# Windowed attention, one core: each block of v spread once in rows of four heads by 32 keys, and the scores' maxima ahead of the sum of the older weights

## The chip, the core and the metric

The kernel runs on one core of one Trainium2 chip. A core has TensorE (matrix products; its weight loads are listed apart as PEld), VectorE (DVE), ScalarE (ACT), GpSimd (POOL) and SyncE (SP, which here only issues DMAs), each with its own instruction list in order. They are held together by semaphores. The metric is the device time of one execution in microseconds. The time before is 4051.28 us, the median of three runs (4048.12 to 4060.52).

## The reference

The input is x of 8 batch elements, 512 tokens, 128 dimensions, with a vector that modulates it. First comes one causal attention layer with 16 heads of 8 dimensions. Then follow six layers, each with a windowed attention and a gated feed-forward part; nearly all of the time, and the whole change but one line, is in the windowed attention:

```
q, k, v = split(x @ Wqkv)           # 16 heads of 64
q, k = rotary(l2norm(q)), rotary(l2norm(k))
# windows of 32 queries; each sees the 32 keys before it and its own 32
sim  = q_w @ [k_(w-1), k_w].T * 8, masked: i < j, i > j + 32, or before the start
out  = softmax(sim) @ [v_(w-1), v_w]          # per head
x   += out @ Wo                     # heads side by side
```

All arithmetic is float32.

## The kernel before

**Units, tiles and steps.** `local_stack` works through 48 units (6 layers by 8 batch elements). A unit has four tiles of 128 tokens (4 windows of 32). One pass of the loop body has four steps, t = 0 to 3, and each step takes a different stage of several tiles: the projections of tile n (`q`, `k`, `v0`, `v1`), the transposes and scores of tile n-1 (`tq`, `tk`, `sim`), the exponential and the normalisation of tile n-2 (`ex`), and the transpose of the weights and the product with v of tile n-3 (`pt`, `z`, `zt`). The feed-forward part of an older unit is spread over the steps: `m1` (means) in step 3, `m2` (variances) in step 0, `h` (three hidden products) in step 1, `y` in step 2. The list `jobs_of` gives TensorE's order in a step: q, tq, k, (ex), tk, v0, pt, sim, v1, z, then m1, m2, h or y, then zt. Each job names the PSUM banks it writes (`q`, `v1`, `pt` in 0 and 1, `v0` in 2 and 3, `z` in 2), and `slot_free` waits until the earlier user of these banks has been taken out.

**Where the work lies.** V is projected with Wo already folded in, so v has 128 columns for each of 16 heads. `v0` and `v1` are two halves of 8 heads, which ScalarE copies to `v_tok` (two buffers, L598, function `copy_v`). TensorE takes rows of 128 in its product with v, and a row is one head and one key. Before, `v_win` (two buffers, `par`) holds for each window 2 heads by 64 keys (the 32 keys before and its own 32) in the 128 partitions, and 8 column blocks; `z` is 8 products per window, one for each pair of heads, 32 per tile.

**SyncE.** `spread_v(u, t)` copies `v_tok` into `v_win` by DMA. Before, each block of 32 keys is written twice, as own keys and as keys before. It waits for both halves of v (`taken`), puts the last 32 keys by in `v_held` (L382, in steps 0 to 2, two issues), waits for `ready["z"]` up to tile n, takes over the older 32 keys from `v_held` (L389, two issues), and issues two times three copies of 64 partitions (L394) and one of 32 (L396). `ready["z"]` starts at 2, so this waits for z of tile n-2. `copy_v` of tile n waits in its turn until the spread of tile n-2 has landed (`win_in`) and, with three tiles of four, until `held_in`. In the last unit of a layer SyncE also loads the next layer's weights in 1 MB pieces: q's and k's ahead of the spread of step 2, v's two ahead of the spread of step 3, each when the last tile has used the old ones (L349), and behind each spread a rotary table (L367).

**VectorE's order in a step.** For q and then k: the sum of squares (L719), the product with the cosines (L723), a clamp (L730, once), two products with the sines (L737, two halves). Then the mask is added to the scores of tile n-1 (L761), then the sum of the weights of tile n-2 (L768), its reciprocal (L770) and the product (L772). In step 1 the gates of the feed-forward part (L749), which wait for ScalarE's gelu; in step 3 the subtraction of the mean (L783), for which ScalarE's square L659 waits. Then the maxima of tile n-1 (L788), the remainder of the next input (L695, steps 0 and 2), the update of x (L799), in step 2 y's (L808).

**ScalarE's order in a step.** Squares of q (L569, L571), the copy of tq, squares of k (L573), k into `k_bd` (L618), the transposed weights (L625), `copy_v(0)`, the logarithm of the norms (L580), the exponential of the scores (L633), the exponential of the norms (L586), in step 1 L640, `copy_v(1)`, the copy of z (L651), then the feed-forward part's pieces: L659 in step 3, three on m2 in step 0, a table load, three gelus and a table load in step 1.

**GpSimd.** It adds the two rotary halves of q and k (L835), refines and applies the norms (L855), and subtracts the maxima from the scores (L883) for the next step's exponential.

**The attention part in front** (`modulated_attention`) also folds Wo into v's weights, one 64-row product per head (`fold`, four groups of four heads; `vt` are the transposed weights, made in steps 2 and 3 of 16, `fold` in steps 7, 7, 11 and 14).

## Time and profile before

| | |
|---|---|
| median of three runs | 4051.28 us |
| the profiled execution, whole | 4061.07 us |
| its span (first to last instruction) | 4059.3 us |
| TensorE busy | 3598.6 us, 89% |
| VectorE busy | 3208.4 us, 79% |
| GpSimd busy | 2756.6 us, 68% |
| ScalarE busy | 2604.8 us, 64% |
| DMA | 512.39 MB, mean 126 GB/s |
| mean granted TensorE clock | 0.974 |

The attention part takes the first 750 us or so, the 48 units the rest, save some 75 us of filling, draining and the last residual. "Busy" is the time in which an engine has an instruction in it; one share over the whole span hides that each step of a unit has its own limit, so the tables below are read by step. Times in a timeline count from the start of the span. In brackets stands how long the engine had been idle before an instruction and what ended that.

### The profile page before, as it was taken

What the parts mean: (1) busy time and instruction counts of PE and PEld (TensorE: products, weight loads), DVE (VectorE), ACT (ScalarE), POOL (GpSimd) and SP (SyncE); (2) the same over time, 40 slices, a digit from 0 to 9 for tenths busy, and PEclk for the clock granted to TensorE, in tenths of its full rate; (3) what the DMA queues carried; (4) which work ended last, traced back from release to release, by engine and by line L of the source; (5) the groups of instructions that cost most, each with busy time, mean ns of one, the idle gap of its engine ahead of it and who ended that gap; (6) DMA issues with size and microseconds to landing.
All of it is one profiled execution on the core that took longest, in us unless ns stands there. A gap on an engine that the chain in (4) does not pass through costs nothing. (4 is left out here: it accounts for less than half of the span.)

```text
span 4059.3 us, 104487 instructions
## 1 busy us (share of the span) xinstructions
PE 3598.6 (89%) x39260; PEld 2658.4 (65%) x39260; DVE 3208.4 (79%) x4352; ACT 2604.8 (64%) x3817; POOL 2756.6 (68%) x2238
## 2 busy tenths in 40 slices
PE   6988888689998999989999989999899998999995
PEld 4666666467666667666766666667576666666663
DVE  5556556588897889887888888888798887888883
ACT  3555555467766676766776767677567676767763
POOL 2344343477777787777777777777677777777772
PEclk9999999799999999999999999999899999999997
DMA  1222220366666666676666676666766667666663
GB/s 47 73 75 90 72 99 16 102 146 133 139 132 164 133 148 134 133 170 133 138 137 132 133 175 139 132 132 142 166 134 137 132 134 174 133 139 134 143 136 88
DMA packets 172730, 512.39 MB, mean 126 GB/s; under 512 B 36862, under 2 KB 56444, under 8 KB 166396
## 3 DMA queue, kind: packets, MB, share of 16 engines
q1 hardware_dynamic: 172668, 511.58, 55.4%
q8 instruction: 37, 0.61, 0.1%
q14 instruction: 25, 0.20, 0.0%
HBM read 51.11 MB, written 32.51 MB: 21 GB/s over the span
## 5 line engine op out<-in xcount | busy, mean ns | idle before, releaser
L460 PE MATMUL st_ps<-st_wqkv,st_xs 128*128 128x512 f32 x4608 | 1273.3, 412 | 99.7 <-DMA st_wqkv<-wqkv_parts 56.3
L835 POOL TENSOR_TENSOR st_qk_rot<-st_qk_rot,st_qk_sq 128x1024 f32<-128x1024 f32 x384 | 912.4, 2381 | 568.4 <-DVE st_qk_sq L737 568.4
L460 PEld LDWEIGHTS st_ps<-st_wqkv,st_xs 128*128 128x128 f32 x4608 | 815.7, 190 | 336.9 <-issue 194.0
L855 POOL TENSOR_TENSOR st_qk_rot<-st_qk_rot,st_rn 128x1024 f32<-128x1024 f32 x384 | 731.2, 1925 | 15.0
L598 ACT ACTIVATE st_v_tok<-st_ps 128x1024 f32<-128x1024 f32 x384 | 389.9, 1015 | 248.5 <-DMA st_v_win<-st_v_tok 244.2
L719 DVE TENSOR_REDUCE st_nt<-st_qk_sq 128x16 f32<-128x1024 f32 x384 | 465.6, 1212 | 78.1 <-ACT st_qk_sq L571 58.1
L737 DVE TENSOR_TENSOR st_qk_sq<-st_ps,st_rot 128x512 f32<-128x512 f32 x768 | 490.0, 678 | 0.0
L723 DVE TENSOR_TENSOR st_qk_rot<-st_ps,st_rot 128x1024 f32<-128x1024 f32 x384 | 467.9, 1219 | 7.5 <-PE st_ps L475 1.6
L500 PE MATMUL st_ps<-st_v_win,st_probT 128*32 128x128 f32 x12288 | 376.1, 274 | 90.1 <-ACT st_v_tok L598 86.7
L1531 DVE TENSOR_REDUCE at_nmx<-at_s 128x1 f32<-128x512 f32 (+3 forms) x512 | 236.7, 485 | 255.1 <-PE at_s L1144 253.8
L500 PEld LDWEIGHTS st_ps<-st_v_win,st_probT 128*32 128x32 f32 x12288 | 325.1, 110 | 165.0 <-issue 155.9
L475 PE MATMUL st_ps<-consts_sb,st_qk_rot 128*128 128x128 f32 x3072 | 402.6, 274 | 11.7 <-POOL st_qk_rot L855 8.2
L475 PEld LDWEIGHTS st_ps<-consts_sb,st_qk_rot 128*128 128x128 f32 x3072 | 353.1, 141 | 87.4 <-issue 47.1
L883 POOL TENSOR_TENSOR st_s<-st_s,st_mx 128x1024 f32<-128x1024 f32 x192 | 374.3, 1949 | 48.7 <-DVE st_mx L788 48.7
L618 ACT ACTIVATE st_k_bd<-st_ps 64x1024 f32<-64x1024 f32 x384 | 389.2, 1013 | 5.1 <-PE st_ps L475 2.9
L1347 ACT ACTIVATE at_probT<-at_t 128x512 f32<-128x512 f32 (+1 forms) x384 | 201.2, 526 | 288.4 <-PE at_t L1163 282.9
L488 PE MATMUL st_ps<-st_k_bd,st_qT 128*32 128x128 f32 x12288 | 377.0, 275 | 2.5 <-ACT st_k_bd L618 2.5
L768 DVE TENSOR_REDUCE st_den<-st_ps 128x16 f32<-128x1024 f32 x192 | 235.0, 1224 | 162.6 <-ACT st_ps L633 160.5
L488 PEld LDWEIGHTS st_ps<-st_k_bd,st_qT 128*32 128x32 f32 x12288 | 325.3, 110 | 36.1 <-issue 31.8
L625 ACT ACTIVATE st_probT<-st_ps 128x1024 f32<-128x1024 f32 x192 | 196.9, 1025 | 231.2 <-PE st_ps L480 231.2
L1614 POOL TENSOR_TENSOR at_qs<-at_q,consts_sb 128x512 fp32r<-128x512 f32 x128 | 131.0, 1041 | 268.6 <-DVE at_q L1477 202.0
L480 PE MATMUL st_ps<-consts_sb,st_s 128*128 128x128 f32 x1536 | 208.9, 280 | 98.9 <-issue 97.7
(149 smaller groups left out, 6154.7 us busy)
## 6 DMA issues: line engine op xcount, KB each, us to landing
st_v_win<-st_v_tok SPq DMA_DIRECT2D x1152, 256.0 KB, 4.6
st_v_win<-st_v_tok SPq DMA_DIRECT2D x384, 128.0 KB, 4.8
st_v_held<-st_v_tok SPq DMA_DIRECT2D x288, 128.0 KB, 4.1
st_v_win<-st_v_held SPq DMA_DIRECT2D x288, 128.0 KB, 2.3
st_wqkv<-wqkv_parts SPq DMA_DIRECT2D x24, 1024.0 KB, 8.5
wqkv_parts<-at_w_parts SPq DMA_DIRECT2D x12, 1024.0 KB, 4.4
wqkv_parts<-at_fold_parts SPq DMA_DIRECT2D x12, 1024.0 KB, 4.6
at_w_raw<-in_wqkv SPq DMA_DIRECT2D x18, 512.0 KB, 5.5
```

The costliest lines, as they stand in the source:

```text
L460: last = pe.matmul(out[:, c * 512:(c + 1) * 512], xs[:, x_part, t * P:(t + 1) * P], wqkv[:, PROJ.index(kind), w_part, c * 512:(c + 1) * 51 ...
L475: last = pe.transpose(out[:, c * P:(c + 1) * P], src[:, c * P:(c + 1) * P], ident)
L488: last = pe.matmul(out[g * WIN:(g + 1) * WIN, c * P:(c + 1) * P], qT[:, par, c * P + g * WIN:c * P + (g + 1) * WIN], k_bd[:, c, :, key:key ...
L500: last = pe.matmul(out[g * WIN:(g + 1) * WIN, 0:P], probT[:, c * P + g * WIN:c * P + (g + 1) * WIN], v_win[:, par, g, c * P:(c + 1) * P], ...
L598: act.activation(v_tok[:, t % 2, a, :], slot_of(f"v{a}", 0, t), ACT.Copy).then_inc(taken[f"v{a}"], 1)
L618: last = act.activation(k_bd[rows, :, a, WIN + t1 * P:WIN + (t1 + 1) * P], src[rows, :, :], ACT.Copy)
L719: dve.tensor_reduce(nt[:, 2 + par, heads], qk_sq[:, cols].rearrange("p (h d) -> p h d", d=DH), AX.X, ALU.add).then_inc(ss_sum, 1)
L723: dve.tensor_tensor(qk_rot[:, cols].rearrange("p (h d) -> p h d", d=DH), slot_of("qk"[a], 0, t).rearrange("p (h d) -> p h d", d=DH), rot[: ...
L737: last = dve.tensor_tensor(dst[:, :, g, :], src[:, :, 1 - g, :], sines.unsqueeze(1).to_broadcast([P, HEADS, DH // 2]), ALU.mult)
L835: pool.tensor_tensor(qk_rot[:, cols], qk_rot[:, cols], qk_sq[:, cols], ALU.add).then_inc(rot_done[a], 1)
L855: pool.tensor_tensor(view, view, rn[:, par, heads_of(a)].unsqueeze(2).to_broadcast([P, HEADS, DH]), ALU.mult).then_inc(normed[a], 1)
L883: pool.tensor_tensor(scores, scores, mx[:, tt % 2, :].unsqueeze(2).to_broadcast([P, HEADS, 2 * WIN]), ALU.subtract).then_inc(shifted, 1)
```

## The change

Four parts.

1. V is spread once. `v_win` has a buffer for each of the four tiles; its 128 partitions are 4 heads by 32 keys, its 4 column blocks the other factor of the 16 heads. `spread_v` issues 16 copies of 32 partitions by 2 KB (64 KB each) per tile, all on `win_in[t]`. `v_held`, its copies and their semaphores are gone. `ready["z"]` starts at 3, so the spread of tile n waits for z of tile n-3. `z` makes 4 products per window with its own keys and then 4 with the keys before, which it reads from the window before, in the same or in the previous tile's buffer; in the first window of a unit these 4 are left out.
2. The scores lie in another order: in each PSUM bank of 512 first the 8 heads' 32 older keys, then the 8 heads' 32 own ones. `sim` reads k in that order (pieces of 32) and writes two pieces of 64. The mask is added from a table of this layout, laid out once at the start. The maxima, the sums and the product are each two instructions of 512, a bank each, and so is GpSimd's subtraction; the reduces run over two dimensions.
3. VectorE takes the maxima straight after the mask add, ahead of the sum, the reciprocal and the product of tile n-2 and of what follows these.
4. Which heads are folded into which columns changes with it; every fold group waits for both halves of the transposed weights.

From top to bottom: the layout's helpers, SyncE's `spread_v`, TensorE's `sim` and `z`, ScalarE's `copy_v` (its two waits on z follow the new start value), VectorE (the start, then the step), GpSimd, and the fold of the attention part.

```diff
-        v_win = sb("v_win", [P, 2, WPT, INNER])
-        v_held = sb("v_held", [P, INNER])
+        v_win = sb("v_win", [P, TILES, WPT, INNER // 2])
+        masks = sb("masks", [P, 2, 512])
...
+    def spread_count(u, d):
+        return u * 256 + 256 * (d + 1)
+    def bank_of(tensor, b):
+        return tensor[:, b * 512:(b + 1) * 512].rearrange("p (s h k) -> p s h k", s=2, h=HEADS // 2)
+    def heads_first(tensor, b):
+        return tensor[:, b * 512:(b + 1) * 512].rearrange("p (s h k) -> p h s k", s=2, h=HEADS // 2)
+    def per_head(tensor, b):
+        half = tensor[:, b * (HEADS // 2):(b + 1) * (HEADS // 2)]
+        return half.unsqueeze(1).unsqueeze(3).to_broadcast([P, 2, HEADS // 2, WIN])
...
-                        for a in range(2):
-                            sp.dma_start(v_held[held_rows(t, a), :], v_tok[P - WIN:P, par, a, :]).then_inc(held_in[par], 16)
                     sp.wait_ge(ready["z"], tiles_done(u, 0, t))
-                        sp.wait_ge(held_in[1 - par], held_count(u, 0, t - 1))
-                        for a in range(2):
-                            sp.dma_start(v_win[a * 2 * WIN:a * 2 * WIN + WIN, par, 0, :], v_held[held_rows(t - 1, a), :])\
-                              .then_inc(carry_in[par], 16)
...
-                        for g in range(1, WPT):
-                            sp.dma_start(v_win[rows, par, g, :], v_tok[(g - 1) * WIN:(g + 1) * WIN, par, a, :])\
-                              .then_inc(win_in[par], 16)
-                        sp.dma_start(v_win[a * 2 * WIN + WIN:(a + 1) * 2 * WIN, par, 0, :], v_tok[0:WIN, par, a, :])\
-                          .then_inc(win_in[par], 16)
+                    for g in range(WPT):
+                        for h in range(4):
+                            sp.dma_start(v_win[h * WIN:(h + 1) * WIN, t, g, :],
+                                         v_tok[g * WIN:(g + 1) * WIN, par, h // 2, h % 2 * 512:h % 2 * 512 + 512])\
+                              .then_inc(win_in[t], 16)
...
-                                            out[g * WIN:(g + 1) * WIN, c * P:(c + 1) * P],
+                                            half[:, :, c % 4 * 2 * WIN:(c % 4 + 1) * 2 * WIN],
                                             qT[:, par, c * P + g * WIN:c * P + (g + 1) * WIN],
-                                            k_bd[:, c, :, key:key + 2 * WIN], start=True, stop=True)
+                                            k_bd[:, c, :, key:key + 2 * WIN].rearrange("p a (s k) -> p s a k", s=2),
...
-                                pe.wait_ge(win_in[par], spread_count(u, d, index))
-                                if index:
-                                    pe.wait_ge(carry_in[par], carry_count(u, d, index))
+                                pe.wait_ge(win_in[index], spread_count(u, d))
+                                for s_part in (1, 0):
+                                    for c in range(4):
+                                        chunk = c // 2 * 4 + s_part * 2 + c % 2
+                                        for g in range(WPT):
+                                            t_win, g_win = divmod(index * WPT + g - 1 + s_part, WPT)
+                                            if t_win < 0:
+                                                continue
+                                            last = pe.matmul(
+                                                out[g * WIN:(g + 1) * WIN, 0:P],
+                                                probT[:, chunk * P + g * WIN:chunk * P + (g + 1) * WIN],
+                                                v_win[:, t_win, g_win, c * P:(c + 1) * P], start=(s_part == 1 and c == 0),
+                                                stop=(c == 3 and (s_part == 0 or index * WPT + g == 0)))
...
-                                act.wait_ge(win_in[t % 2], spread_count(u, d2, t2))
-                                if t2 < TILES - 1:
-                                    act.wait_ge(held_in[t2 % 2], held_count(u, d2, t2))
+                                act.wait_ge(win_in[t2], spread_count(u, d2))
...
+                for i in range(2):
+                    dve.tensor_copy(masks[:, i, :].rearrange("p (s h k) -> p s h k", s=2, h=HEADS // 2),
+                                    mask[i].rearrange("p (s k) -> p s k", s=2).unsqueeze(2).to_broadcast([P, 2, HEADS // 2, WIN]))\
+                       .then_inc(masked, 1)
...
-                                              mask[0 if t1 == 0 else 1].unsqueeze(1).to_broadcast([P, HEADS, 2 * WIN]),
+                                              masks[:, t1 > 0, :].unsqueeze(1).to_broadcast([P, 2, 512]),
                                               ALU.add).then_inc(taken["sim"], 1)
+                        if alive(u, d1):
+                            dve.wait_ge(taken["sim"], n - 1)
+                            for b in range(2):
+                                last = dve.tensor_reduce(mx[:, t1 % 2, b * 8:b * 8 + 8], heads_first(s[:, t1 % 2, :], b), AX.XY, ALU.max)
+                            last.then_inc(max_ready, 1)
                         if alive(u, d2):
                             dve.wait_ge(ready["ex"], n - 2)
-                            dve.tensor_reduce(den[:, t2 % 2, 0, :], weights, AX.X, ALU.add).then_inc(den_ready, 1)
+                            for b in range(2):
+                                last = dve.tensor_reduce(den[:, t2 % 2, 0, b * 8:b * 8 + 8], heads_first(weights, b), AX.XY, ALU.add)
...
+                            for b in range(2):
+                                last = dve.tensor_tensor(bank_of(s[:, t2 % 2, :], b), bank_of(weights, b),
+                                                         per_head(den[:, t2 % 2, 1, :], b), ALU.mult)
+                            last.then_inc(taken["ex"], 1)
...
-                        if alive(u, d1):
-                            dve.wait_ge(taken["sim"], n - 1)
-                            dve.tensor_reduce(mx[:, t1 % 2, :], scores, AX.X, ALU.max).then_inc(max_ready, 1)
...
-                for a in range(2):
-                    pool.memset(v_win[a * 2 * WIN:a * 2 * WIN + WIN, 0, 0, :], 0.0).then_inc(v_zeroed, 1)
-                pool.sem_inc(ready["z"], 2)
+                pool.sem_inc(ready["z"], 3)
...
+                            for b in range(2):
+                                scores = bank_of(s[:, tt % 2, :], b)
+                                last = pool.tensor_tensor(scores, scores, per_head(mx[:, tt % 2, :], b), ALU.subtract)
...
-                        rows, half = slice(g // 2 * DH, (g // 2 + 1) * DH), g % 2
-                        pe.wait_ge(taken["vt"], count(b, 0, 2, half))
+                        rows = slice(g % 2 * DH, (g % 2 + 1) * DH)
+                        pe.wait_ge(taken["vt"], count(b, 0, 2, 1))
...
-                            c = TILES * half + i
+                            c = 2 * i + g // 2
```

## Rows read from the trace of the kernel before

**Rows 1.** Busy time by window, one unit: window, length, then busy time and count per engine.

```profile
2014.60:2080.30 65.70, 61.10 (x730) 45.06 (x730) 57.65 (x73) 46.18 (x65) 51.53 (x41) 1.00 0.64 136
```

**Rows 2.** List of waits, whole run: who waits, for whom, us in total, times, longest.

```profile
ACT st_v_tok L598 <- DMA st_v_win<-st_v_tok: 244.2, 137, 3.4
...
DVE st_den L768 <- ACT st_ps L633: 160.5, 138, 2.9
...
ACT st_xc L659 <- DVE st_xc L783: 99.3, 48, 7.6
...
PE st_ps L500 <- ACT st_v_tok L598: 86.7, 92, 2.0
...
PE st_ps L460 <- DMA st_wqkv<-wqkv_parts: 56.3, 8, 11.1
```

**Rows 3.** Timeline, VectorE, each step's first L719: start, us, instruction, [idle before].

```profile
2010.85 1.22 DVE L719 TENSOR_REDUCE st_nt<-st_qk_sq 128x16 f32<-128x1024 f32 x1 [0.32 <-DVE xT_sb L808]
...
2025.21 1.22 DVE L719 TENSOR_REDUCE st_nt<-st_qk_sq 128x16 f32<-128x1024 f32 x1 [0.30 <-ACT st_qk_sq L571]
...
2040.85 1.21 DVE L719 TENSOR_REDUCE st_nt<-st_qk_sq 128x16 f32<-128x1024 f32 x1
...
2060.89 1.22 DVE L719 TENSOR_REDUCE st_nt<-st_qk_sq 128x16 f32<-128x1024 f32 x1 [0.66 <-ACT st_qk_sq L571]
...
2076.57 1.22 DVE L719 TENSOR_REDUCE st_nt<-st_qk_sq 128x16 f32<-128x1024 f32 x1 [0.32 <-DVE xT_sb L808]
```

**Rows 4.** Timeline of steps 0 and 1: what waits behind the spread.

```profile
2033.21 1.02 ACT L598 ACTIVATE st_v_tok<-st_ps 128x1024 f32<-128x1024 f32 x1 [2.02 <-DMA st_v_win<-st_v_tok]
...
2035.30 1.23 DVE L768 TENSOR_REDUCE st_den<-st_ps 128x16 f32<-128x1024 f32 x1 [1.59 <-ACT st_ps L633]
...
2034.47 1.95 PE L500 MATMUL st_ps<-st_v_win,st_probT 128*32 128x128 f32 x64 [0.95 <-ACT st_v_tok L598]
...
2050.08 1.95 PE L500 MATMUL st_ps<-st_v_win,st_probT 128*32 128x128 f32 x64 [0.93 <-ACT st_v_tok L598]
```

**Rows 5.** Timeline of step 2, VectorE: pair, mask add, sum, reciprocal, product.

```profile
2066.98 1.28 DVE L737 TENSOR_TENSOR st_qk_sq<-st_ps,st_rot 128x512 f32<-128x512 f32 x2
2068.18 1.21 DVE L761 TENSOR_TENSOR st_s<-st_ps,consts_sb 128x1024 f32<-128x1024 f32 x1
2069.44 1.23 DVE L768 TENSOR_REDUCE st_den<-st_ps 128x16 f32<-128x1024 f32 x1
2070.70 0.25 DVE L770 RECIPROCAL st_den<-st_den 128x16 f32<-128x16 f32 x1
2070.99 1.23 DVE L772 TENSOR_TENSOR st_s<-st_ps,st_den 128x1024 f32<-128x1024 f32 x1
```

**Rows 6.** Lines L389 and L396, SP's issues: duration in ns, least, median, most.

```profile
L389 SPq DMA_DIRECT2D st_v_win<-st_v_held x288: 507/534/601, 788.1 to 3976.7; - x144
...
L396 SPq DMA_DIRECT2D st_v_win<-st_v_tok x384: 598/1018/1997, 773.0 to 3983.4; - x192
```

**Rows 7.** Timeline of step 3: mask add, subtraction of the mean, ScalarE's square of it.

```profile
2018.13 1.21 DVE L761 TENSOR_TENSOR st_s<-st_ps,consts_sb 128x1024 f32<-128x1024 f32 x1
...
2022.60 0.68 DVE L783 TENSOR_TENSOR st_xc<-xT_sb,st_ps 128x512 f32<-128x512 f32 x1
...
2023.32 0.63 ACT L659 ACTIVATE st_xc<-st_xc 128x512 f32<-128x512 f32 x1 [1.94 <-DVE st_xc L783]
```

**Rows 8.** Timeline across a change of layer, SP and TensorE.

```profile
1257.29 1.62 PE L460 MATMUL st_ps<-st_wqkv,st_xs 128*128 128x512 f32 x6
...
1275.78 1.64 PE L460 MATMUL st_ps<-st_wqkv,st_xs 128*128 128x512 f32 x6 [1.45 <-DMA st_wqkv<-wqkv_parts]
...
1279.63 0.94 SPq L349 DMA_DIRECT2D st_wqkv<-wqkv_parts  x2
...
1289.30 2.90 PE L460 MATMUL st_ps<-st_wqkv,st_xs 128*128 128x512 f32 x6 [11.01 <-DMA st_wqkv<-wqkv_parts]
...
1300.64 1.64 PE L460 MATMUL st_ps<-st_wqkv,st_xs 128*128 128x512 f32 x6
```

More of the change, by code:

```diff
@@ L264, in local_stack @@
         wqkv_in = {k: sem(f"w{k}_in") for k in PROJ}
-        win_in = [sem("win_in0"), sem("win_in1")]
-        carry_in = [sem("carry_in0"), sem("carry_in1")]
-        held_in = [sem("held_in0"), sem("held_in1")]
-        zeroed, shift_zeroed, v_zeroed, rot_in = sem("zeroed"), sem("shift_zeroed"), sem("v_zeroed"), [sem(f"rot_in{t}") for t in range(TILES)]
+        win_in = [sem(f"win_in{t}") for t in range(TILES)]
+        masked = sem("masked")
+        zeroed, shift_zeroed, rot_in = sem("zeroed"), sem("shift_zeroed"), [sem(f"rot_in{t}") for t in range(TILES)]
         KINDS = (*PROJ, "tq", "tk", "pt", "sim", "ex", "z", "zt", "m1", "m2", "h", "y")
@@ L487, in unit @@
                                         key = index * P + g * WIN
+                                        half = out[g * WIN:(g + 1) * WIN, c // 4 * 512:c // 4 * 512 + 512].rearrange("p (s x) -> p s x", s=2)
                                         last = pe.matmul(
-                                            out[g * WIN:(g + 1) * WIN, c * P:(c + 1) * P],
+                                            half[:, :, c % 4 * 2 * WIN:(c % 4 + 1) * 2 * WIN],
                                             qT[:, par, c * P + g * WIN:c * P + (g + 1) * WIN],
-                                            k_bd[:, c, :, key:key + 2 * WIN], start=True, stop=True)
+                                            k_bd[:, c, :, key:key + 2 * WIN].rearrange("p a (s k) -> p s a k", s=2),
+                                            start=True, stop=True)
@@ L492, in unit @@
                             elif kind == "z":
                                 pe.wait_ge(taken["pt"], tiles_done(u, d, index))
-                                pe.wait_ge(win_in[par], spread_count(u, d, index))
-                                if index:
-                                    pe.wait_ge(carry_in[par], carry_count(u, d, index))
-                                for c in range(IC):
-                                    for g in range(WPT):
-                                        last = pe.matmul(
-                                            out[g * WIN:(g + 1) * WIN, 0:P],
-                                            probT[:, c * P + g * WIN:c * P + (g + 1) * WIN],
-                                            v_win[:, par, g, c * P:(c + 1) * P], start=(c == 0), stop=(c == IC - 1))
+                                pe.wait_ge(win_in[index], spread_count(u, d))
@@ L646, in unit @@
                         if alive(u, d3):
[L648 removed]
+                            act.wait_ge(ready["z"], n)
                             if not (start and n < 5):
@@ L753, in unit @@
                         d1, t1 = divmod(t - 1, TILES)
-                        scores = s[:, t1 % 2, :].rearrange("p (h k) -> p h k", h=HEADS)
                         if alive(u, d1):
@@ L760, in unit @@
                                 dve.wait_ge(ready["pt"], n - 3)
[L761 to L762 removed]
+                            dve.tensor_tensor(s[:, t1 % 2, :].rearrange("p (b x) -> p b x", b=2),
+                                              slot_of("sim", d1, t1).rearrange("p (b x) -> p b x", b=2),
+                                              masks[:, t1 > 0, :].unsqueeze(1).to_broadcast([P, 2, 512]),
                                               ALU.add).then_inc(taken["sim"], 1)
+                        if alive(u, d1):
[3 more added lines that the diff above has]
+                            last.then_inc(max_ready, 1)
                         if alive(u, d2):
                             dve.wait_ge(ready["ex"], n - 2)
[L767 to L768 removed]
+                            weights = slot_of("ex", d2, t2)
+                            for b in range(2):
+                                last = dve.tensor_reduce(den[:, t2 % 2, 0, b * 8:b * 8 + 8], heads_first(weights, b), AX.XY, ALU.add)
+                            last.then_inc(den_ready, 1)
                             dve.wait_ge(den_ready, 2 * (n - 2) - 1)
@@ L817, in _ @@
             def _(pool):
-                for a in range(2):
-                    pool.memset(v_win[a * 2 * WIN:a * 2 * WIN + WIN, 0, 0, :], 0.0).then_inc(v_zeroed, 1)
-                pool.wait_ge(v_zeroed, 2)
-                pool.sem_inc(ready["z"], 2)
+                pool.sem_inc(ready["z"], 3)
                 pool.wait_ge(small_in, 64)
```

31 lines of the change are left out of this document (3 added, 28 removed).

## The prediction

> **What bounds the kernel now.** I read the table of busy time by window first, then the list of waits, then the timeline of one unit (one of 48 passes over a layer and a batch element), engine by engine, and last the timeline across a change of layer. In one unit of 65.7 us TensorE is busy 61.1, VectorE 57.7 and ScalarE 46.2 [rows 1]. No engine is full, so the step length is set by a loop that runs through several engines, and the reader has to find the place where each step is held up.
>
> I measure a step from the start of VectorE's first reduce (L719 on q) to the same instruction of the next step: 14.36 us in step 3, 15.64 in step 0, 20.04 in step 1 and 15.68 in step 2, together 65.72 [rows 3]. The loop is this: VectorE's three instructions on q free the banks in which TensorE then puts `pt`; TensorE runs `pt`, `sim`, `v1`, `z`, the feed-forward product of that step, `zt` and the next `q`; ScalarE squares that q; VectorE reduces it. VectorE's own list is the second loop, and the longer one decides.
>
> Where the DMA stands in it: `copy_v(0)` on ScalarE waits 244.2 us over the run until the spread of tile n-2 has landed. Behind this wait queue the exponential of the scores, for which VectorE's sum then waits (160.5 us), and the release of bank 2, for which TensorE's `z` waits (86.7 us) [rows 2]. In step 0 the copy is 2.02 us late, VectorE's sum 1.59 and `z` 0.95; in step 1 `z` is 0.93 late [rows 4]. In step 2 nothing waits for the DMA, and VectorE is full: only 0.32 us of idle stands before its next L719 [rows 3]. In step 3 the copy is late, but `z` isn't.
>
> **Spreading v once, four tiles kept.** SP's condition changes from "z of tile n-2 done" to "z of tile n-3 done". z of tile n-3 runs in step n itself, so the spread starts a whole step earlier. Sixteen issues follow. The nearest row is the copy of 32 partitions from v_held, median 0.534 us per issue; the other is the last quarter of the old spread, 1.018 us, issued behind a backlog of 256 KB copies [rows 6]. I take 0.57 with the gap between two, since the new pieces (64 KB) are smaller than both and leave no backlog: 16 x 0.57 = 9.1 us per step of 14.6 us or more. Landing comes one more step ahead of the copy that waits for it. So the waits of ScalarE on this DMA go, all of them.
>
> What is late next, step by step. Step 0: `z` starts 0.95 us earlier, with it `m2`, and ScalarE's three instructions on it, its squares and L719: with some 0.08 us that TensorE's weight load waits beside it, 15.64 becomes 14.61. VectorE's own list must fit under this (below: 14.28, it does, with 0.3 us to spare). Step 1: `z` 0.93 us earlier, with it the three h products, the two table loads and gelus; with some 0.07 beside it 20.04 becomes 19.04. The maxima stood in the gap in which VectorE waits for gelu, and there is room left without them.
>
> **VectorE's order and its halved instructions.** Three 1024-wide instructions become pairs of 512. A pair with no wait between is L737, 1.28 us, against 1.21 for one 1024-wide [rows 5]: +0.07 each. L737 reads runs of 32 like the new forms, so I add nothing for the order of the elements. The maxima now stand straight behind the mask add that they depend on. A dependent pair costs 1.26 from start to start (sum, then reciprocal), the reciprocal and the product 0.29, and one without a dependence some 0.12 less than 1.26 [rows 5]. The block was mask 1.26, sum 1.26, reciprocal 0.29, product 1.14, maxima 1.13, in all 5.08 us when nothing waits; it becomes mask 1.25, maxima 1.20, sum 1.32, reciprocal 0.29, product 1.20, in all 5.26: +0.18 per tile. Bounds: 0 (a pair as dear as one), and +0.15 per pair if each half costs an unoverlapped 0.68 us; no row shows a reduce over two dimensions or with a gap, so its upper end is open and is a rival below.
> The Trainium skill ("VectorE: DVE Perf Modes", "The DRAIN you can't avoid") says that the next instruction cannot start before the pipe is empty and that the count of instructions should be kept low, which speaks against halving. The trace has the overlapped pair at +0.07 us [rows 5]; by the page it would be nearer the +0.15, and the sum some 10 us less good.
>
> Step 2 is VectorE's own: 15.68 + 0.19 = 15.87. Step 0: the mask add 7.29 after L719 [rows 3, 5], the block 5.26, and what follows it in the list (the update of x, the remainder of the next input): from the sum to the next L719 it was 2035.30 to 2040.85 without idle [rows 3, 4], 5.55, less sum, reciprocal, product and maxima (3.82), 1.73. Together 14.28.
>
> **Where the new order hurts.** In step 3 VectorE subtracts the mean (L783) for ScalarE's L659, which stands ahead of ScalarE's squares of the next q; L659 waits 99.3 us over 48 units [rows 2], 1.94 each time [rows 7]. Before, L783 stood behind the product and ahead of the maxima. Now the maxima are ahead of it: from the mask add to L783 it is 5.26 us where it was 4.47 with the 0.58 us of idle that the DMA caused (the mask add at 2018.13, L783 at 2022.60 [rows 7]). L783, L659, the squares and L719 are all 0.79 us later: 14.36 becomes 15.15. TensorE is not what ends that step, so its slack doesn't help.
>
> A unit: 15.15 + 14.61 + 19.04 + 15.87 = 64.67 against 65.72, 1.05 us less, times 48 = 50 us.
>
> **The change of layer.** At five of them TensorE waits for new weights, 56.3 us in all [rows 2], 11.3 each. SP issues v's weights only at 1279.63, because it sits in `spread_v` waiting for `z` of the current step, and then issues ten copies; TensorE starts on them at 1289.30, 9.7 us later [rows 8]. The granted clock is at its lower level (1.2 GHz) behind this wait: six products took 2.90 us against 1.64 a step on [rows 8], and by the same ratio, for part of their time, `pt` and `sim` lose another 1.3, so 2.6. Some 1.7 us of wait would be there without the weights (TensorE's `pt` waits for VectorE's L737 in any case), so a change costs 11.3 + 2.6 - 1.7 = 12.2 us. Now SP's wait is over long before. q's weights go out when q of tile 3 is done (1257.29 + 1.62 [rows 8] = 1258.9), k's 2.3 us on (1261.2), the sixteen spreads until 1270.5, the table and v's at 1271.4: 8.2 us earlier. TensorE starts on v at 1281.1; without the 1.45 us for k's weights [rows 8] and with the 1 us that `pt` waits anyway it would lose nothing until 1277.6. That leaves 3.5 us, and half of the low clock's 2.6, since the wait is a third as long: 4.8. 12.2 - 4.8 = 7.4 us, times 5 = 37. Bounds: 1 us each (issues at 1.018), 12 each.
>
> **The rest.** `sim` and `z` have the same counts, save 4 products fewer in tile 0, where TensorE waits anyway: nothing. `sim` now reads in four pieces of 32 and writes in two of 64; it already reads in two of 64 at the price of z's contiguous 128, so nothing, and up to 0.2 us per step (25 us) as a bound. GpSimd's shift in halves: like VectorE's pairs, +0.07 to 0.15 us a step; GpSimd is busy 51.5 of 65.7 us [rows 1], and its last piece of the step, the shift, is wanted only by the next step's exponential: nothing. The two mask tables cost VectorE a pair, 1.3 us, once. In the attention part the fold waits for both halves of the transposed weights, four steps after the second was made: nothing. GpSimd's two memsets went: nothing.
>
> Sum: -50 - 37 + 1 = -86 us. The profiled execution took 4061.07 us (span 4059.3), the median of the runs is 4051.28, 9.8 less: 4061 - 86 = 3975 profiled, 3965 for the median.
>
> **Rivals.**
> 1. The subtraction isn't late (VectorE catches up, or ScalarE's squares were not what ended step 3): 48 x 0.79 = 38 us more gain, 3927. For it: only one step of four. Against: L659's wait is in every unit. 0.13.
> 2. The wait on the DMA was covered: next limits stand close behind in steps 0 and 1 (GpSimd's normalising of q, the slots), the +0.79 and +0.19 eat what little goes, and only the layers' changes gain: 4051 - 37 = 4014. For it: `z` waits only in half the steps, 86.7 us in all. 0.15.
> 3. The issues keep their price of 1.018 us at the changes of layer only: 4051 - 50 - 5 = 3996. 0.07.
> 4. SP becomes the bound: at 1.018 + 0.04 us each, 64 issues take 67.7 us per unit, against the 65.72 of now: +2.0 x 48 = 96 us, 4147, slower. It decides from 0.98 us an issue. For it: the 1.018 row is a 32-partition copy too. Against: that row follows copies of 256 KB, and 0.534 is seen without these [rows 6]. 0.05.
> The Trainium skill ("DMA: Bandwidth & Descriptors", "Measured") has 64 KB transfers at 0.95 us and calls those below 64 KB dominated by descriptors; that is for another path, and would put SP just under this bound, with a time near 3996 or worse.
> 5. The new access patterns are dear: a reduce over two dimensions with a gap costs VectorE 0.6 us or more than one over 64 in a row, twice per step. +1.2 us is in full on steps 3 and 2, 0.9 on step 0, 0.6 on step 1, together 3.9 us x 48 = 187: 4152, slower. It decides from some 0.3 us per reduce. 0.08.
>
> My forecast holds 0.52. A difference counts as one from 0.3%, 12 us, on. Faster: 0.52, 0.13, 0.07 and 0.12 of rival 2 make 0.84, of which I take 0.03 off for what no row shows (the length of the loops' code, for one), 0.81; same: rival 2's other 0.03 and 0.02 of these, 0.05; slower: rivals 4 and 5 and the last 0.01, 0.14. The range of 8 in 10 reaches from rival 1 to a little past rival 2.
>
> **What would show it.** Right: no wait of L598 on a DMA; L768 without idle; `z` without a wait on ScalarE; L659's wait 2.7 us instead of 1.94, and step 3 at 15.1 while steps 0 and 1 are 1 us shorter; the SP issue near 0.55; TensorE's wait for st_wqkv some 20 us in all instead of 56. Wrong: an L768 or maxima pair above 1.4 us, `sim` above 2.1, SP's queue without gaps, or a step 3 of 14.4.

## The result and the profile after

The changed kernel takes 3945.97 us (median of four runs, 3941.92 to 3950.02) against 4051.16 for the kernel before beside it: ratio 0.9737, interval 0.9716 to 0.9757, 105 us less. The forecast was 3965. The profiled execution took 3942.58 us, 118.5 less than the 4061.07 of before.

From the page: the span, the busy times, the DMA, and the copies of v and of the weights (size of each, median us from issue to landing; before, the copies of v were 256 and 128 KB and took 4.6 and 4.8 us, the weights 8.5).

```profile
span 3940.8 us, 104815 instructions
...
PE 3568.8 (91%) x38876; PEld 2641.1 (67%) x38876; DVE 3285.9 (83%) x4930; ACT 2611.0 (66%) x3817; POOL 2784.8 (71%) x2428
...
DMA packets 181947, 285.96 MB, mean 73 GB/s; under 512 B 52222, under 2 KB 71804, under 8 KB 175612
...
st_v_win<-st_v_tok SPq DMA_DIRECT2D x3072, 64.0 KB, 2.0
st_wqkv<-wqkv_parts SPq DMA_DIRECT2D x24, 1024.0 KB, 7.0
```

The list of waits answers to [rows 2]. No wait of `copy_v` (now L584) on a DMA is in it; the sum (now L766) waits for ScalarE once; the wait of L645 (the L659 of before) has grown, as forecast.

```profile
ACT st_xc L645 <- DVE st_xc L783: 134.5, 48, 6.7
...
PE st_ps L442 <- DMA st_wqkv<-wqkv_parts: 8.2, 6, 2.3
...
DVE st_den L766 <- ACT st_ps L619: 2.7, 1, 2.7
```

One unit by window, as [rows 1], and VectorE's first reduce of each step (L719 is now L710), as [rows 3].

```profile
2003.34:2068.29 64.95, 61.00 (x723) 45.06 (x722) 59.35 (x84) 46.31 (x65) 52.15 (x46) 1.00 0.28 65
```

```profile
2003.34 1.22 DVE L710 TENSOR_REDUCE st_nt<-st_qk_sq 128x16 f32<-128x1024 f32 x1 [1.03 <-ACT st_qk_sq L559]
...
2019.03 1.22 DVE L710 TENSOR_REDUCE st_nt<-st_qk_sq 128x16 f32<-128x1024 f32 x1 [0.32 <-DVE xT_sb L804]
...
2034.18 1.22 DVE L710 TENSOR_REDUCE st_nt<-st_qk_sq 128x16 f32<-128x1024 f32 x1 [1.44 <-ACT st_qk_sq L559]
...
2049.27 1.21 DVE L710 TENSOR_REDUCE st_nt<-st_qk_sq 128x16 f32<-128x1024 f32 x1
...
2068.29 1.22 DVE L710 TENSOR_REDUCE st_nt<-st_qk_sq 128x16 f32<-128x1024 f32 x1 [1.03 <-ACT st_qk_sq L559]
```

| step | before | forecast | after |
|---|---|---|---|
| 3 | 14.36 | 15.15 | 15.15 |
| 0 | 15.64 | 14.61 | 15.09 |
| 1 | 20.04 | 19.04 | 19.02 |
| 2 | 15.68 | 15.87 | 15.69 |
| unit | 65.72 | 64.67 | 64.95 |

Here are VectorE's pairs in step 3, and ScalarE behind them: the maxima and the sum take 1.28 us a pair, with the reciprocal between sum and product, and the mean's subtraction L783 comes 5.25 us after the mask add. ScalarE waits 2.72 us for it, then squares q, and only then can L710 start.

```profile
2026.32 1.21 DVE L751 TENSOR_TENSOR st_s<-st_ps,st_masks 128x1024 f32<-128x1024 f32 x1
...
2027.57 1.28 DVE L759 TENSOR_REDUCE st_mx<-st_s 128x8 f32<-128x512 f32 x2
...
2028.76 1.28 DVE L766 TENSOR_REDUCE st_den<-st_ps 128x8 f32<-128x512 f32 x2
...
2030.07 0.25 DVE L769 RECIPROCAL st_den<-st_den 128x16 f32<-128x16 f32 x1
...
2030.36 1.29 DVE L772 TENSOR_TENSOR st_s<-st_ps,st_den 128x512 f32<-128x512 f32 x2
...
2031.57 0.68 DVE L783 TENSOR_TENSOR st_xc<-xT_sb,st_ps 128x512 f32<-128x512 f32 x1
...
2032.28 0.64 ACT L645 ACTIVATE st_xc<-st_xc 128x512 f32<-128x512 f32 x1 [2.72 <-DVE st_xc L783]
```

The change of layer, SyncE first and then TensorE (answers to [rows 8]). SyncE is no longer held by `z`; v's weights are issued at 1252.41, and TensorE's v0 starts at 1258.00 with 1.64 us of idle and at the full clock (1.63 us for its six products).

```profile
1238.66 2.59 SPq L348 DMA_DIRECT2D st_wqkv<-wqkv_parts  x2
1241.71 10.04 SPq L377 DMA_DIRECT2D st_v_win<-st_v_tok  x16
1251.79 0.58 SPq L366 DMA_DIRECT2D st_rot<-rotary_tables  x1
1252.41 0.93 SPq L348 DMA_DIRECT2D st_wqkv<-wqkv_parts  x2
```

```profile
1255.33 1.04 PE L457 MATMUL st_ps<-consts_sb,st_qk_rot 128*128 128x128 f32 x8
1258.00 1.63 PE L442 MATMUL st_ps<-st_wqkv,st_xs 128*128 128x512 f32 x6 [1.64 <-DMA st_wqkv<-wqkv_parts]
1259.47 1.04 PE L462 MATMUL st_ps<-consts_sb,st_s 128*128 128x128 f32 x8
```

**Where the time came from.** I measure from one `pt` to the `pt` four steps on. The five stretches with a change of layer fell from 394.0 us in all to 326.6: 67.4 us, which is 12.7 each beyond an ordinary unit's share. The first four stretches lost 10.2 together (3.2 of it ordinary); the late spread below gives this back, so it comes from the earlier start of the spread. The other 38 stretches lost 29.5, 0.78 each, and what follows the last of them 3.7. The attention part in front lost 7.7; two runs with the same code there (the changed kernel and the first experiment) began their first `pt` at 798.95 and 806.72, so that is no effect of the change, and it is most of why the profiled pair differs by more than the medians. The changes of layer scatter too: in two runs below that keep the old spread, the five stretches took 384.5 and 388.6 us, not 394.0. Up to 2 us of the 12.7 can be such scatter.

### The profile page after: what moved, and what is told of

Its sections match the earlier page's. It is cut to its first block and busy times, and to the rows that moved or that the text cites. A ratio compares the mean times of both kernels' runs of the same rounds, so it can differ in the third digit from the quotient of the medians.

```text
span 3940.8 us, 104815 instructions
## 1 busy us (share of the span) xinstructions
PE 3568.8 (91%) x38876; PEld 2641.1 (67%) x38876; DVE 3285.9 (83%) x4930; ACT 2611.0 (66%) x3817; POOL 2784.8 (71%) x2428
## 5 line engine op out<-in xcount | busy, mean ns | idle before, releaser
L848 POOL TENSOR_TENSOR st_qk_rot<-st_qk_rot,st_rn 128x1024 f32<-128x1024 f32 x384 | 731.9, 1927 | 15.0
L710 DVE TENSOR_REDUCE st_nt<-st_qk_sq 128x16 f32<-128x1024 f32 x384 | 466.0, 1213 | 136.4 <-ACT st_qk_sq L559 121.6
L877 POOL TENSOR_TENSOR st_s<-st_s,st_mx 128x512 f32<-128x512 f32 x384 | 404.1, 1073 | 6.0 <-DVE st_mx L759 6.0
L584 ACT ACTIVATE st_v_tok<-st_ps 128x1024 f32<-128x1024 f32 x384 | 388.0, 1010 | 3.2 <-PE st_ps L442 3.1
L462 PEld LDWEIGHTS st_ps<-consts_sb,st_s 128*128 128x128 f32 x1536 | 165.9, 141 | 204.5 <-issue 203.0
```

Source lines behind the costliest of these rows:

```text
L584: act.activation(v_tok[:, t % 2, a, :], slot_of(f"v{a}", 0, t), ACT.Copy).then_inc(taken[f"v{a}"], 1)
L710: dve.tensor_reduce(nt[:, 2 + par, heads], qk_sq[:, cols].rearrange("p (h d) -> p h d", d=DH), AX.X, ALU.add).then_inc(ss_sum, 1)
L848: pool.tensor_tensor(view, view, rn[:, par, heads_of(a)].unsqueeze(2).to_broadcast([P, HEADS, DH]), ALU.mult).then_inc(normed[a], 1)
L877: last = pool.tensor_tensor(scores, scores, per_head(mx[:, tt % 2, :], b), ALU.subtract)
```

## The experiments

Times are medians; each ratio is to the kernel before on the same chip. Unit lengths are from the profiled run of each.

**The maxima put back in the changed kernel**

```diff
 # VectorE, changed kernel
-    (mask add) (maxima) (sum, reciprocal, product) (gates) (mean's subtraction)
+    (mask add) (sum, reciprocal, product) (gates) (mean's subtraction) (maxima)
```

> The changed kernel with the maxima put back to their old place, behind the subtraction of the mean; the layout, the halves and the single spread stay. Theory A (mine): with the DMA wait gone, the exponential is ready when the mask add ends, so the sum can follow at once and the early maxima gain nothing; in step 3 they delay the subtraction for which ScalarE waits. Step 3 goes from 15.15 to 14.4 us, the others stay: 48 x 0.75 = 36 us less than 3946, so 3910. Rival B: the early maxima fill a wait of VectorE for the exponential, and without them step 0, 1 and 2 each grow by up to 1.2 us: 3946 + 48 x 1 to 3, 4000 or more. Rival C: neither matters, 3946 within 10.

Measured: 3902.96 us, ratio 0.9637 (0.9622 to 0.9653), 43 us less than the changed kernel. Step 3 is 14.01 instead of 15.15, the unit 63.78. ScalarE waits 1.58 us for the mean instead of 2.72, the same 1.14:

```profile
2014.76 1.03 ACT L619 ACTIVATE st_ps<-st_s 128x1024 f32<-128x1024 f32 x1 [0.56 <-DVE st_qk_sq L728]
...
2019.39 0.63 ACT L645 ACTIVATE st_xc<-st_xc 128x512 f32<-128x512 f32 x1 [1.58 <-DVE st_xc L777]
```

The forecast's 0.79 for this step was right against the step of before, but that step still held 0.58 us of wait for the DMA. Against the changed kernel with its old order the loss is 1.14. Over 48 units that would be 55 us, and the stretches from `pt` to `pt` do fall by 51.5; in this profiled run the attention part, whose code is the same, took 7.8 us longer, and the medians, 43 apart, hold such scatter too.

**The same reordering alone, in the kernel before**

```diff
 # VectorE, kernel before
+    maxima (dve.tensor_reduce(mx...)) ahead of the sum
-    maxima behind the mean's subtraction
```

> The kernel before with one part of the change alone: the maxima moved up, straight behind the mask add, ahead of the sum. Theory A (mine): it fills time in which VectorE waits for the exponential anyway (0.58 to 1.59 us in steps 3, 0 and 1), so these steps don't gain, since they end with ScalarE or GpSimd; in step 3 the subtraction of the mean comes 0.6 us later and the step grows by 0.6 us, in step 2 by 0.1: 48 x 0.7 = 34 us more than before, 4085. Rival B: the early maxima are a gain by themselves where the wait on the DMA is still there: 4051 - 20 or less. Rival C: the 1.14 us per unit that they cost in the changed kernel are their price here too: 4051 + 55 = 4106.

Measured: 4048.15 us, ratio 0.9988 (0.9974 to 1.0002), no change to be told; my figure, 4085, was wrong. The steps say why: 14.95, 15.0, 20.2 and 15.69 against 14.36, 15.64, 20.04 and 15.68. Step 3 loses 0.59, and step 0 gains as much. There `copy_v` still waits for the DMA and the exponential behind it is late; VectorE used to stand idle for 1.59 us before the sum [rows 4], and now the maxima fill that hole. The list of waits of this run: the copy's wait is there as before, the sum's has gone from 160.5 to 9.4, and L719 waits 173.6 us for the squares.

```profile
DVE st_nt L719 <- ACT st_qk_sq L571: 173.6, 134, 2.7
...
DVE st_den L772 <- ACT st_ps L633: 9.4, 8, 2.7
```

**The spread one step later, in the changed kernel**

```diff
-                pool.sem_inc(ready["z"], 3)
+                pool.sem_inc(ready["z"], 2)
 # and ScalarE's two waits on z one lower
```

> The changed kernel with the spread held back by one step: it waits for z of tile n-2 again instead of n-3, with the four buffers, the single spread and half the bytes kept. Theory A (mine): the gain comes from the earlier start, not from the bytes, since 16 issues of 0.63 us take as long as the old ten. The spread then lands some 12 us after z, ScalarE's copy_v(0) waits for it again some 1 to 2 us per step and the weights of v come late at a change of layer: 4030 to 4060. Rival B: half the bytes are what took the wait away, and the time stays at 3946 within 15.

Measured: 4013.47 us, ratio 0.9910 (0.9894 to 0.9926). That is 67 us more than the changed kernel, and all of it lies elsewhere than I said: an ordinary unit is 64.92 us, unchanged. The five stretches with a change of layer are 74.6 to 76.3, some 10 more each, and the first four units 14 more together. `copy_v` waits for the DMA again, but 0.21 to 0.83 us at a time instead of 1 to 2, and that is about what the exponential behind it waits for VectorE anyway (0.55 to 1.04 in the changed kernel).

```profile
ACT st_v_tok L584 <- DMA st_v_win<-st_v_tok: 102.3, 137, 3.7
...
PE st_ps L442 <- DMA st_wqkv<-wqkv_parts: 48.3, 6, 10.0
```

So with this order of VectorE the ordinary unit doesn't need the earlier start. The single spread, half the bytes in copies that land in 2.0 us instead of 4.6, brings the copy's wait from 244.2 us over the run [rows 2] down to 102.3, and what is left of it is covered. The earlier start pays at the changes of layer and at the beginning. Whether the bytes or the size of each copy count wasn't separated.

**Both of these together**

```diff
 # changed kernel with the late spread, and the maxima back behind the mean
```

> The changed kernel with the spread held back by one step (as in the second experiment, where the ordinary unit kept its 64.92 us although ScalarE's copy waited 0.6 to 0.8 us for the DMA) and the maxima in their old place (the first experiment, 63.78 us per unit). Theory A (mine): what is left of the DMA wait was covered by the slack that the early maxima made; with the maxima late the exponential is wanted earlier, and a part of the 0.6 to 0.8 us shows: a unit of 64.2 to 64.8 us, the changes of layer 10 us each: 3903 + 67 + 30 = 4000. Rival B: the late spread costs an ordinary unit nothing in either order, unit 63.8, time 3970.

Measured: 3983.2 us, ratio 0.9839 (0.9814 to 0.9863). Unit 64.17: step 3 is 14.0, but step 0 is 15.4 and not 15.07, since the sum waits for ScalarE again, 81.8 us over the run. The time lies between my figure and the rival's (4000 and 3970). In this order the earlier start is worth 0.39 us in each ordinary unit (63.78 against 64.17); the early maxima had hidden that. With the late spread the early maxima cost 30 us, with the early spread 43, and in the kernel before they cost nothing. The less VectorE waits for the exponential, the less there is for them to fill.

**v's weights behind the last spread**

```diff
-                            for kind in (("q", "k"), ("v0", "v1"))[t - (TILES - 2)]:   # ahead of spread_v(u, t)
+                            for kind in ("v0", "v1"):                                 # behind spread_v(u, TILES - 1)
```

> The changed kernel with the loads of the next layer's v weights put behind the last tile's spread instead of ahead of it, 16 issues or 10 us later. It measures what the place of these loads in SyncE's list is worth. Theory A (mine): the whole gain at a change of layer (12.7 us each) comes from when these loads are issued. Issued 10 us later, TensorE waits 1.6 + 10 us for them and the low clock costs 1 to 3 us more: 5 x 10 to 13, 3946 + 57 = 4003. Rival B: TensorE's wait is covered for the most part by another loop, under 20 us in all: 3966 or less.

Measured: 4002.44 us, ratio 0.9881 (0.9858 to 0.9905), 56 us more, 11.3 for each change of layer. Ordinary units stay at 64.91. SyncE and TensorE at the first change:

```profile
1256.64 0.58 SPq L366 DMA_DIRECT2D st_rot<-rotary_tables  x1
1257.34 10.01 SPq L377 DMA_DIRECT2D st_v_win<-st_v_tok  x16
1267.39 1.07 SPq L348 DMA_DIRECT2D st_wqkv<-wqkv_parts  x2
```

```profile
1272.55 2.90 PE L447 MATMUL st_ps<-st_wqkv,st_xs 128*128 128x512 f32 x6 [11.42 <-DMA st_wqkv<-wqkv_parts]
```

The sixteen issues take 10.0 us and stand in front; the wait is 11.42 us and the clock falls to its lower level behind it (2.90 us for six products). From the issue to the products it is 5.0 to 5.2 us here and 5.0 to 5.6 in the changed kernel. In the kernel before it was 9.7 at this change [rows 8], and 9.4, 6.5, 11.5 and 6.8 at the other four. This is the third of them, then the fifth in the changed kernel, the only one there with the lower clock behind the wait:

```profile
2359.08 0.86 SPq L349 DMA_DIRECT2D st_wqkv<-wqkv_parts  x2
...
2365.62 2.90 PE L460 MATMUL st_ps<-st_wqkv,st_xs 128*128 128x512 f32 x6 [9.59 <-DMA st_wqkv<-wqkv_parts]
```

```profile
3336.43 2.71 PE L442 MATMUL st_ps<-st_wqkv,st_xs 128*128 128x512 f32 x6 [2.25 <-DMA st_wqkv<-wqkv_parts]
```

**Halves alone, in the kernel before**

```diff
-    dve.tensor_reduce(mx, scores, ...)          # and the sum, and the product: 1024 at once
+    for b in range(2): ...                      # 512 each, old layout, old order
```

> The kernel before with the maxima, the sum and the product of the weights each in two instructions of 512 instead of one of 1024, layout and order as before. Theory A (mine): each pair costs 0.07 us more on VectorE; three pairs, 0.2 us per step, which counts only in step 2, where VectorE's list is full: 48 x 0.2 = 10 us, 4061. Rival B (the page's rule that every instruction pays an emptying of the pipe): 0.15 us a pair, 22 us, 4073. Rival C: not to be told from no change.

Measured: 4049.72 us, ratio 1.0003 (0.9986 to 1.0019). The steps are 14.5, 15.6, 20.0 and 15.69. My 10 us aren't there. The pairs do take 0.07 us more each (the maxima 1.27, then the remainder's subtraction), but step 2, the one that I called full, doesn't grow (15.69 and 15.68). In exchange the subtraction shrinks: 0.74 us here, where it took 0.91 before.

```profile
1996.60 1.27 DVE L793 TENSOR_REDUCE st_mx<-st_s 128x8 f32<-128x512 f32 x2
1997.79 0.74 DVE L695 TENSOR_TENSOR st_xs<-xT_sb,st_xs 128x256 fp32r<-128x256 f32 x1
```

**The remainder moved from step 0 to step 1**

```diff
+                        if t == 1 and alive(u, 0) and alive(u, -1):   # ahead of the gates
+                            remainder_half(u, 0, 1)
-                        if t == 0 and alive(u, 0) and alive(u, -1):   # last but one in the step
-                            remainder_half(u, 0, 1)
```

> The changed kernel with the remainder of the next input that stood at the end of step 0 put into step 1, ahead of the gates, where VectorE waits for gelu. In step 0 it took 2.01 us and ended 0.27 us after GpSimd's normalising instruction beside it, against 0.69 to 0.74 elsewhere. Theory A (mine): a VectorE instruction with two inputs in SBUF doesn't start while GpSimd's instruction runs, so step 0 ends with GpSimd; moved, step 0 falls from 15.09 to 14.6 (ScalarE's squares), 48 x 0.45 = 22 us: 3924. Rival B: GpSimd's own chain (tq waits for its normalising) holds step 0 anyway and the time stays within 8 us of 3946, with the wait moved to another instruction. Rival C: it is late in step 1 and TensorE's q of step 2 waits: slower.

Measured: 3909.67 us, ratio 0.9651 (0.9637 to 0.9665), 36 us less than the changed kernel. Step 0 is 14.39, the forecast's 14.61 and better; step 1 is 18.8. That is 14 us less than the 3924 expected: I had step 0 at 14.6 and no gain in step 1. In step 1 the subtraction takes 1.15 us, but there it lies in VectorE's wait for the gelu.

**Is it held, or slowed? GpSimd's multiplications in halves**

The remainder's subtraction (L681) takes 0.74 us in step 2 and 2.01 in step 0; its shortest of 96 is 0.42. In both steps GpSimd's two multiplications (L848) run beside it:

```profile
2015.89 0.74 DVE L681 TENSOR_TENSOR st_xs<-xT_sb,st_xs 128x256 fp32r<-128x256 f32 x1
...
2047.33 2.01 DVE L681 TENSOR_TENSOR st_xs<-xT_sb,st_xs 128x256 fp32r<-128x256 f32 x1
```

```profile
2014.44 3.95 POOL L848 TENSOR_TENSOR st_qk_rot<-st_qk_rot,st_rn 128x1024 f32<-128x1024 f32 x2
...
2045.30 3.77 POOL L848 TENSOR_TENSOR st_qk_rot<-st_qk_rot,st_rn 128x1024 f32<-128x1024 f32 x2
```

In step 0 the first multiplication ends at 2047.20 (the records taken one by one), the second at 2049.07; the subtraction starts at 2047.33 and ends at 2049.34, 0.28 after the second. In step 2 the first multiplication ends at 2016.34, and the subtraction ends 0.28 after that, at 2016.62. It is so everywhere: in the twelve traces of this case 1078 of these subtractions took longer than 0.5 us, and every one ends 0.28 or 0.29 us after a GpSimd instruction. GpSimd is held in turn: the multiplication that follows in step 2 takes 2.09 us instead of 1.91, so the pair takes 3.95 where it is 3.77 in the other steps.

```diff
-    pool.tensor_tensor(view, view, rn..., ALU.mult)                      # 128 x 1024
+    for b in range(2): pool.tensor_tensor(view[:, hs, :], ..., ALU.mult)  # 128 x 512 each
```

> The changed kernel, with each of GpSimd's two multiplications that normalise q and k (128 x 1024, 1.9 us each, two per tile) split into two of half the columns. It asks why the remainder's subtraction of step 0 takes 2.01 us beside them and 0.74 in step 2. If that VectorE instruction is held until GpSimd's running instruction ends, it is held for the rest of an instruction of half the length: it starts 0.14 us after the second multiplication, so it should end some 1.0 us earlier, about 1.1 us long; step 0 goes from 15.09 to some 14.3 and the time to 3946 - 0.8 x 48 = 3907, less if the two extra instructions per tile (0.1 to 0.2 us for GpSimd) make tq wait longer: then up to 3925. The rival is that both engines merely share a memory path, each slowed while the other runs: the bytes are the same, the subtraction stays at 2.0 us and the time at 3946 or a little more.

Measured: 3920.7 us, ratio 0.9688 (0.9668 to 0.9708), 25 us less than the changed kernel. The subtraction is down to 1.29 us and step 0 to 14.39:

```profile
2036.11 4.23 POOL L850 TENSOR_TENSOR st_qk_rot<-st_qk_rot,st_rn 128x512 f32<-128x512 f32 x4
...
2038.15 1.29 DVE L681 TENSOR_TENSOR st_xs<-xT_sb,st_xs 128x256 fp32r<-128x256 f32 x1
```

The bytes that GpSimd moves are the same and it takes longer over them (4.05 us instead of 3.77 where no subtraction stands beside them, 4.23 here), yet the other engine gets through sooner: the subtraction starts 0.04 us into the third half and ends 0.28 after it. That speaks against a shared bandwidth and for a hold until the running instruction ends. The median is 14 us above my 3907: step 0 is 14.39 where I had 14.3, and step 2 grew from 15.69 to 15.79. There the subtraction waited for a whole multiplication and now waits for two halves, which take a little longer (it is 0.90 us).

**The two gains together, without and with the halves**

```diff
 # changed kernel, maxima back behind the mean, remainder in step 1
+# and in the second: GpSimd's multiplications in halves
```

> Both of the above: the maxima back in their old place and the remainder in step 1. Theory A: the two gains are in different steps and add up, 3946 - 36 - 22 = 3888, with steps of 14.4, 14.6, 19.0 and 15.7 us. Rival B: step 0 with late maxima is held by something else, the gains don't add, about 3910.

> The same split of GpSimd's multiplications, in the version that has both earlier edits (maxima back behind the subtraction of the mean, the second half of the remainder in step 1). There no long hold of the remainder stands on the path of step 0 any more, so by the theory of the hold the split has little left to give: 3863, within 10, or a few us slower from GpSimd's extra instructions. If instead shorter GpSimd instructions helped the whole chain (its results handed on sooner), this version would gain as much as the other, some 0.5 us a unit and more: below 3840.

Measured: 3863.22 us, ratio 0.9544 (0.9527 to 0.9561), and 3871.79, ratio 0.9562 (0.9540 to 0.9584). The gains add up: 43 and 36 us apart, 83 together (I had expected 3888, from smaller gains). The steps are 14.01, 14.39, 18.8 and 15.68, the unit 62.87. The halves bring nothing more where the hold is off the path, as expected. The first is the best version that was run, 2.1% under the changed kernel. VectorE is busy 58.85 of its 62.87 us:

```profile
2003.00:2065.87 62.87, 60.83 (x725) 45.05 (x724) 58.85 (x85) 46.52 (x64) 52.15 (x46) 1.00 0.29 67
```

## Why the prediction came out as it did

**The DMA wait goes, and `z` and the gates come earlier: right, for another reason in part.** Steps 1 and 3 came out within 0.02 us and L645's wait at 2.72 us where 2.7 was forecast. But I put the end of the wait down to the spread that starts a step earlier. The late spread kept the ordinary unit at 64.92, so there the single spread is enough; only with the maxima late does the earlier start show in an ordinary unit, 0.39 us. No issue is dear: 0.63 us from one to the next, 16 in 10.1 us, where I had taken 0.57. The rivals with SyncE as the bound and with issues of 1.018 us fell.

**Step 0, mis-sized by 0.48 us.** The failed step is "Together 14.28": VectorE's list should have fitted under the 14.61 set by `z`. The 1.73 us that I carried over for the update of x and the remainder came from the step of before, in which the subtraction took 1.20 us (2039.73 to 2040.93), since GpSimd's second multiplication was half over. With `z` and the sum 1 us earlier, VectorE reaches the subtraction earlier too, runs into the start of the second multiplication and stands until it ends. The rest of the sum was right: 14.28 and the 0.81 us more of this one instruction make 15.09. 0.74, 1.20 and 2.01 us are one instruction with different amounts of waiting in it, and 0.42 is what it takes alone. So VectorE's list became the bound of this step after all. Moving the instruction (step 0 to 14.39) and halving what it waits for (14.39 too) both show it. By 0.48 x 48 this is 23 us of gain not had.

The Trainium skill has this mechanism ("SBUF — State Buffer", "Who interferes with whom"): a VectorE instruction with both inputs in SBUF contends with a GpSimd instruction that reads SBUF, and the second to issue blocks fully until the first is done. The subtraction is such an instruction, and the trace agrees (it ends 0.28 us behind the multiplication). It is the rule that I should have weighed here.

**Step 2, 0.18 too long, by the same mechanism.** I added 0.19 for the pairs to a list that I called full. The block did grow, but behind it stands the same subtraction, and in the kernel before it ended 0.28 us after GpSimd's first multiplication just as after. It starts 0.19 later and takes 0.17 less (0.74 for 0.91), the next L719 is 15.69 behind the last. What ends step 2 is GpSimd's multiplication, by way of the hold, and VectorE had 0.2 us of slack that looked like busy time.

**The early maxima: right in size against before, incomplete as a judgement.** +0.79 in step 3 came true to the hundredth. What I didn't ask is what the same edit does without the other. In the kernel before it fills a wait and costs nothing; once the single spread has removed the wait it costs 43 us. The change undid the use of its own second half.

**The change of layer, mis-sized: 7.4 forecast, 12.7 measured.** That is 63 us instead of 37. The step that failed is "TensorE starts on v at 1281.1": I kept the 9.7 us from issue to products [rows 8]. It was one change of five, between 6.5 and 11.5 us, all behind ten copies of up to 256 KB on the same queue; behind sixteen of 64 KB it is 5.0 to 5.6. With 4.1 us less, 1.64 us of wait remain, and in four of five changes the clock no longer falls (six products in 1.62 or 1.63 us, 2.71 in the fifth), so the low clock's price goes too. The weights' median landing went from 8.5 to 7.0 us. What is left of a change is 0.4 us beyond an ordinary unit, where the forecast had 4.8; what it cost before was 13.1, where I had 12.2, and that part is within the scatter of the runs. Why half the bytes in smaller copies in front let the weights land sooner wasn't tested.

**The sum.** Forecast: 50 + 37 - 1 = 86 us. Found in the profiled pair: 38 (0.78 to 0.80 x 48) for the ordinary units, 63 for the layers, 7 for the start, 7.7 in the attention part that are run-to-run, and some 3 at the end of the run that I didn't follow up. 12 too much, 26 too little and the 7 of the start, which I had at nothing, leave 21 us, about the 19 between 3965 and 3946. That the time came out so near is in part luck: the two errors in size have opposite signs. The access patterns cost nothing: the maxima and sums over two dimensions with a gap take 1.28 us a pair, as L737 did with plain runs [rows 5].

## What to carry to other kernels

When a change removes a wait, look again at every reordering that was worth something because it filled that wait: here the early maxima were neutral before and cost 43 us after. A time from issue to use, and the duration of an instruction that shares something with another engine, belong to what was running beside them; work them out anew for the order that the change makes. When one instruction has several durations in the timeline (0.42, 0.74, 1.20, 2.01), find out why before one of them goes into a sum.

## What the runs showed of the hardware

- A VectorE subtraction with two inputs in SBUF doesn't slow down beside GpSimd, it waits for the end of GpSimd's running instruction: 0.42 us at its shortest, 2.01 when it meets a 1.9 us multiplication at its start, 1.29 when that is split in two, and in step 1 of the best version 2.34. It ends 0.28 us behind the GpSimd instruction, and the wait counts as busy time of VectorE.
- Small differences in arrival decide between the extremes: in the kernel before with the early maxima the subtraction of step 0 takes 0.42 to 0.47 us in 33 of 48 units and 2.17 or 2.18 in 9. In the 9 it starts 0.03 or 0.04 us before the end of the first multiplication, in all but the first of the 33 it starts 0.04 to 0.19 us before it. One unit of each kind:

```profile
2026.91 3.77 POOL L855 TENSOR_TENSOR st_qk_rot<-st_qk_rot,st_rn 128x1024 f32<-128x1024 f32 x2
2028.78 2.18 DVE L695 TENSOR_TENSOR st_xs<-xT_sb,st_xs 128x256 fp32r<-128x256 f32 x1
...
2565.24 4.04 POOL L855 TENSOR_TENSOR st_qk_rot<-st_qk_rot,st_rn 128x1024 f32<-128x1024 f32 x2
2567.09 0.42 DVE L695 TENSOR_TENSOR st_xs<-xT_sb,st_xs 128x256 fp32r<-128x256 f32 x1
```

- The time from the issue of 1 MB of weights to the first product that uses them was 6.5 to 11.5 us behind copies of up to 256 KB (five changes of layer in the kernel before), and 5.0 to 5.6 behind copies of 64 KB (ten changes in two runs).
- SyncE issues copies of 64 KB at one in 0.63 us, in ordinary steps and at the change of layer (sixteen in 10.0 us, 11.1 at most); no backlog like that behind the 1.018 us of before [rows 6] came up.
